# Last attention: four buffers per kind, residual two groups behind, and a wait on GpSimd every fourth group

## The chip, the cores and the metric

The kernel runs on one NeuronCore of a Trainium2 chip, alone. The metric is the device time in microseconds of one execution, the median of the runs shown. Before the change it is 2379.06 us, the median of 3 runs (2378.51 to 2380.45).

## What is computed

Four graph layers in a row on 50,000 nodes of 128 features and 25,000 edges sorted by destination. Each layer is followed by a residual sum and a layer norm, `x = layernorm(x + layer(x))`. The last layer is an attention with one head:

```
h = x @ W
alpha = leaky_relu(att_l . h[dst] + att_r . h[src])
a = exp(alpha - segment_max(alpha, dst)[dst]); a = a / (segment_sum(a, dst)[dst] + 1e-16)
out = segment_sum(h[src] * a, dst) + bias
x = layernorm(x + out)
```

## The kernel before

The kernel works on edges in NG = 49 groups of 512 (GT = 4 tiles of 128 edges), the last layer like the others. It is a row of stages with a barrier of all engines between them. In the profiled execution they lie about as follows: preparation to 68 us, stage a (gathers of source rows, statistics, first logits) to 642, softmax and b to 794, c to 1130, a softmax to 1166, d (second half of the first layer) to 1345, e (second layer) to 1674, f (third layer) to 2045, g (gathers and logits of the last layer, and the rows of nodes without edges) to 2366, and h (the last attention) to the end. Most of the change lies in stage h; the wait on GpSimd lies in the helper that stages f and h share.

In stage h each group g passes these steps, written by helpers as a software pipeline. `pipeline(eng, stages)` takes pairs (lag, step) and, for each g in order, has the engine issue every step for group g - lag in the order of the list.

- **weighing** (VectorE, L1207): the source rows times their attention weight, into `msg[:, s]`, with s = g % 2. The rows of 28 groups lie in SBUF; those of the other 21 come from DRAM through `ring`.
- **turning** (TensorE, L1334): four transposes of `msg` into `bank[s]`.
- **scanning** (VectorE, L1222): a segmented running sum from `bank[s]` into `G[:, s]`, which starts from the other slot's first column.
- **project** (TensorE, L1686 and L1690): a bias row by a matmul with one row of weights (L1686), then the sum times W3 (L1690), into `bank[2 + s]`.
- **residual** (VectorE, L1674): `z[:, s] = bank[2 + s] + rload[:, j]`, j = g % 4. The old node rows `rload` come by SP's load (L1719), issued four groups ahead once `z` has freed its slot.
- **norm_stats, norm_var** (L696, L705), ScalarE's root (L738), **norm_rate** and **norm_shift** (L714, L722), then ScalarE's apply (L742) into `outr[:, j]`, one of four output slots.
- **scatter** (GpSimd, L686): four indirect DMAs of 128 rows each, from `outr[:, j]` to the output. ScalarE writes a slot again only when the scatters of four groups earlier have landed (`h_sc{j}`).

VectorE's order of one step is scan of g, rate of g-2, weighing of g+1, shift of g-2, residual, stats and variance of g-1. TensorE's is turning of g, project of g-1. There are two slots each of `msg`, `G`, turned bank, row bank and `z`. Stage d has the same pipeline with 64 columns in place of 128, its output stored by SP and not scattered. Stage f scatters each group to a DRAM table by the same GpSimd helper `attend_pool`.

Of the kernel before, what the change touches and what calls it, by code (L numbers as in the profile page):

```python
# [15 lines left out]
P = 128  # L16
# [8 lines left out]
GT = 4  # L25
# [30 lines left out]
def program(nc, x, src, dst, ea, W1, al1, ar1, b1, W2, al2, ar2, b2, L1W, L1b,  # L56
# [21 lines left out]
    with ExitStack() as ctx:  # L78
# [182 lines left out]
        def S(name):  # L261
            return sem_of(shared(name)[0])
# [37 lines left out]
        def wait(eng, name, n):  # L300
            sem_name, start = shared(name)
            eng.wait_ge(sem_of(sem_name), n + start)
            if eng is nc.sync and not isinstance(n, int):
                pause(eng)
# [28 lines left out]
        def pipeline(eng, stages, between=(), ahead=0):  # L333


            least, most = min(lag for lag, _ in stages), max(lag for lag, _ in stages)
            parts = len(between)
            ends = {-ahead + RING * (1 + (BODIES - 1) * (n + 1) // parts): between[n] for n in range(parts)}
            for g in range(least, NG + most):
                if g in ends:  # L340
                    ends[g]()
                for lag, stage in stages:
                    if 0 <= g - lag < NG:
                        stage((g - lag) // RING, (g - lag) % RING)

        def count(eng, name, i, j, lag=0, per=1):

            n = RING * i + j + 1 - lag
            if isinstance(n, int) and n <= 0:
                return  # L350
            wait(eng, name, n * per)
# [332 lines left out]
        def scatter(pool, frm, table, kind, g, done):  # L684
            for c in range(GT):
                nc.gpsimd.indirect_dma_start(  # L686
                    table, bass.IndirectOffsetOnAxis(ap=idx[:, kind, (g + 1) * GT + c:(g + 1) * GT + c + 1].bitcast(U32), axis=0), frm(c), None,
                    bounds_check=N - 1, oob_is_err=False).then_inc(done, 16)
# [991 lines left out]
        def attend_tensor(pe, tag, width, W, b):  # L1680
            def project(i, j):
                s = j % 2
                count(pe, tag + "_scan", i, j)
                count(pe, tag + "_z", i, j, 2)
                if b:
                    nc.tensor.matmul(bank[2 + s][:], ones[0:1, 0:P], brow, start=True, stop=False)  # L1686

                k = width if b else width + 1
                for c in range(GT):
                    ins = nc.tensor.matmul(bank[2 + s][:, c * F:(c + 1) * F], G[0:k, s, c * P:(c + 1) * P], W[:],  # L1690
                                           start=not b, stop=not b or c == GT - 1)
                ins.then_inc(S(tag + "_mm"), 1)
            wait(pe, tag + "_ones", 1)
            pipeline(pe, [(0, turning(pe, tag, width)), (1, project)])
# [10 lines left out]
        def attend_pool(pool, tag, table, kind, rev):  # L1705
            def step(i, j):
                g = RING * i + j
                count(pool, tag + "_row", i, j)
                scatter(pool, lambda c: outr[:, j, c, :], table, kind, NG - 1 - g if rev else g, S(f"{tag}_sc{j}"))
            at_tiles(step)  # L1710
            for j in range(RING):
                wait(pool, f"{tag}_sc{j}", GT * 16 * (BODIES + (j == 0)))

        def linear_sync(sp, tag, table, to, rev, used, more=None, also=()):

            def load(i, j):
                g = RING * i + j
                count(sp, tag + used, i, j, RING)
                sp.dma_start(rload[:, j].rearrange("p t f -> p (t f)"), edge_row(table, NG - 1 - g if rev else g)) \  # L1719
                    .then_inc(S(f"{tag}_ld{j}"), 16)  # L1720

            def rows(i, j):

                g = RING * i + j
                if g < NR:
                    return
                if g >= NR + RING:
                    count(sp, tag + "_msg", i, j, RING)
                sp.dma_start(ringf[:, j, 0, :], edge_row(more, NG - 1 - g if rev else g)) \
                    .then_inc(S(f"{tag}_xs{j}"), 16)  # L1730

            def store(i, j):
                g = RING * i + j
                count(sp, tag + "_row", i, j)
                sp.dma_start(edge_row(to, NG - 1 - g if rev else g), outf[:, j, :]).then_inc(S(f"{tag}_out{j}"), 16)
            if more is None:
                pipeline(sp, [(-2, load)] + ([(3, store)] if to is not None else []) + list(also))
            else:
                pipeline(sp, [(-2, rows), (-2, load)])
            if to is not None:  # L1740
                for j in range(RING):
                    wait(sp, f"{tag}_out{j}", 16 * (BODIES + (j == 0)))
# [354 lines left out]
        def g_sync(sp):  # L2097
# [31 lines left out]
            for s in range(OQ):  # L2129
                sp.wait_ge(S(f"go_out{s}"), 32 * len(range(s, NQD, OQ)))  # L2130

        block = ctx.enter_context(nc.Block())

        @block.sync
# [46 lines left out]
        @block.tensor  # L2181
        def _(pe):
            prep_tensor(pe)
            barrier(pe)
            a_tensor(pe)
            barrier(pe)
            softmax_tensor(pe, 0, HEADS, feat[:, :, HF:FW], wide, None)
            b_tensor(pe)
            barrier(pe)
            c_tensor(pe)  # L2190
            barrier(pe)
            softmax_tensor(pe, 1, 1, logit[:, :, 0:1], slim, (last,), own)
            barrier(pe)
            attend_tensor(pe, "d", HF, W2_s, 0)
            barrier(pe)
            e_tensor(pe)
            barrier(pe)
            f_tensor(pe)
            barrier(pe)
            g_tensor(pe)  # L2200
            barrier(pe)
            softmax_tensor(pe, 2, 1, logit4, slim, (first,), own4)
            attend_tensor(pe, "h", P, W3_s, 1)
            barrier(pe)

        @block.scalar
# [24 lines left out]
        @block.vector  # L2231
        def _(v):
            prep_vector(v)
            barrier(v)
            a_vector(v)
            barrier(v)
            softmax_vector(v, 0, HEADS, wide, None, None, alpha[:, :, 0:HEADS])
            b_vector(v)
            barrier(v)
            c_vector(v)  # L2240
            barrier(v)
            softmax_vector(v, 1, 1, slim, (last,), None, alpha[:, :, 0:1])
            barrier(v)
            attend_vector(v, "d", feat, HF, False)
            barrier(v)
            e_vector(v)
            barrier(v)
            f_vector(v)
            barrier(v)
            g_vector(v)  # L2250
            barrier(v)
            softmax_vector(v, 2, 1, slim, (first,), 1e-16, alpha[:, :, 0:1])
            attend_vector(v, "h", None, P, True)
            barrier(v)


# [23 lines left out]
```

## Time and profile before

| | us |
|---|---|
| median of the timed runs | 2379.06 (2378.51 to 2380.45) |
| span of the profiled execution | 2740.2 |
| busy: TensorE matmuls | 1916.0 (70%) |
| busy: VectorE | 1686.4 (62%) |
| busy: GpSimd | 1374.4 (50%) |
| busy: ScalarE | 1075.7 (39%) |

The profiled execution is 361 us longer than the timed ones. Busy times are sums over a span in which the stages have different limits, so what bounds stage h has to be read from its own stretch. TensorE's ends are modelled in a profile and its starts are recorded. Where the profile can't name what ended a wait, it writes "remote" or "another core or an unknown queue"; there is only one core here.

### The profile page before, as it was taken

To read this page: it belongs to the slowest core of one execution; us is meant where nothing else is said; L and a number is where in the kernel's file an instruction comes from. 1 tells how busy PE (TensorE), PEld (TensorE's weight loads), DVE (VectorE), ACT (ScalarE), POOL (GpSimd) and SP (SyncE) were. 2 spreads that over 40 slices of the span, in tenths; PEclk is the share of its full clock that TensorE was granted. 3 is DMA by queue.
4 is the path that set the end of the run, shared out by engine and by line. 5 is a ranking of instruction groups with operands and counts; after the bars stand their busy time and mean duration, and the time that the engine had idled before them with its cause. 6 is when DMAs were issued, how large, how long until landed. Compare 5 with 4: busy or idle time off the path is not lost.

```text
span 2740.2 us, 31801 instructions
## 1 busy us (share of the span) xinstructions
PE 1916.0 (70%) x7812; PEld 1275.1 (47%) x7812; DVE 1686.4 (62%) x6502; ACT 1075.7 (39%) x2966; POOL 1374.4 (50%) x1389
## 2 busy tenths in 40 slices
PE   1788888886556776577545556999965777567573
PEld 1677777886432222166444444666541211244342
DVE  3544444446866666499657776999863655655553
ACT  0222222221654444445334443666653444232222
POOL 4566666650015555300266660677665666256555
PEclk9656555556777667555577777999985555555555
DMA  3444544445356554344466553335426887422331
GB/s 78 144 138 137 136 130 129 138 137 197 132 200 188 167 155 142 106 139 150 131 188 174 163 169 105 127 129 148 136 71 223 312 281 262 144 73 74 99 103 38
DMA packets 273498, 403.75 MB, mean 147 GB/s; under 512 B 98887, under 2 KB 115424, under 8 KB 273060
## 3 DMA queue, kind: packets, MB, share of 16 engines
q1 hardware_dynamic: 216108, 308.88, 34.9%
q0 software_dynamic: 43904, 76.05, 10.8%
q10 hardware_dynamic: 13304, 16.80, 1.7%
q8 instruction: 65, 1.06, 0.2%
q14 instruction: 117, 0.96, 0.1%
HBM read 223.76 MB, written 185.49 MB: 149 GB/s over the span
## 4 chain that ended last, share of the span: by engine, by line
DVE 21%; issue 15%; ACT 9%; PE 6%; another core or an unknown queue 6%; POOL 0%; DMA 0%; SPq 0%; ACTq 0%; DVEq 0%; POOLq 0%
ACT outr L742 4%; DVE G L1222 4%; DVE stats L696 4%; DVE msg L2048 3%; DVE z L1674 2%; ACT big L1947 2%; DVE z L1826 2%; DVE mv L705 1%; PE bank L1690 1%; ACT big L1955 1%; PE bank L1686 1%; DVE z L1834 1%; ACT hT L1933 1%; DVE xT L1523 1%
## 5 line engine op out<-in xcount | busy, mean ns | idle before, releaser
L680 POOL DMA_INDIRECT ring<-in_x_dram,idx x392 | 373.3, 952 | 228.5 <-issue 96.3
L680 POOL DMA_INDIRECT ring<-x_t,idx x280 | 268.4, 959 | 370.2 <-SPq L313 209.0
L742 ACT ACTIVATE outr<-z,rn 128x128 f32<-128x128 f32 x784 | 322.6, 483 | 252.7 <-DVE rn L722 105.4
L680 POOL DMA_INDIRECT ring<-hidden_e,idx x196 | 192.4, 982 | 303.3 <-DVE idx L1548 166.4
L686 POOL DMA_INDIRECT x_t<-outr,idx x196 | 235.3, 1201 | 172.7 <-ACT outr L742 94.1
L686 POOL DMA_INDIRECT out_dram<-outr,idx x196 | 193.6, 988 | 186.0 <-ACT outr L742 129.7
L2078 PE MATMUL bank<-DB,z 20*128 20x512 f32 x196 | 201.9, 1131 | 76.9 <-DVE xT L1523 29.7
L1106 DVE COPY cross<-bank 128x32 f32<-128x32 f32 x49 | 9.4, 191 | 318.0 <-remote 294.3
L1334 PE MATMUL bank<-ident,msg 128*64 128x128 f32 (+1 forms) x392 | 102.9, 417 | 145.7 <-DVE msg L1207 138.8
L1004 PE MATMUL bank<-bT,msg 128*128 128x4 f32 x784 | 153.1, 318 | 73.6 <-ACT msg L1046 68.0
L1690 PEld LDWEIGHTS bank<-W_s,G 65*128 65x128 f32 (+1 forms) x784 | 169.6, 318 | 69.5 <-issue 67.1
L1222 DVE TENSOR_TENSOR_SCAN G<-cont,G,bank 128x512 f32<-128x512 uint8 (+1 forms) x144 | 179.7, 1248 | 27.2 <-remote 21.6
L1004 PEld LDWEIGHTS bank<-bT,msg 128*128 128x128 f32 x784 | 147.8, 281 | 90.2 <-ACT msg L1046 84.5
L1690 PE MATMUL bank<-W_s,G 65*128 65x128 f32 (+1 forms) x784 | 187.4, 417 | 0.4 <-DVE G L1222 0.4
L696 DVE BATCH_NORM_STATS2 stats<-z 128x6 f32<-128x128 f32 x784 | 171.1, 281 | 5.1
L738 ACT ACTIVATE sd<-mv,epsc 128x4 f32<-128x4 f32 x196 | 57.8, 295 | 286.4 <-DVE mv L705 155.6
L1538 DVE SCALAR_TENSOR_TENSOR msg<-iota,shi,bank 128x391 bf16<-128x391 f16 x196 | 113.6, 619 | 91.2 <-PE bank L1498 40.1
L1674 DVE TENSOR_TENSOR z<-bank,ring 128x512 f32<-128x512 f32 x98 | 67.0, 683 | 127.2 <-remote 85.0
L1334 PEld LDWEIGHTS bank<-ident,msg 128*64 128x64 f32 (+1 forms) x392 | 64.4, 188 | 168.4 <-DVE msg L1207 152.6
L1497 PE MATMUL bank<-table,hT 128*128 128x391 bf16 x196 | 81.7, 417 | 81.4 <-issue 37.0
L1786 PE MATMUL bank<-ident,outr 128*128 128x128 f32 x196 | 41.5, 350 | 137.1 <-ACT hT L1862 56.9
L680 POOL DMA_INDIRECT big<-x_t,idx x112 | 106.6, 952 | 57.9 <-issue 31.6
(404 smaller groups left out, 4647.1 us busy)
## 6 DMA issues: line engine op xcount, KB each, us to landing
hT<-in_x_dram SPq DMA_DIRECT2D x194, 256.0 KB
x_t<-outr SPq DMA_DIRECT2D x98, 256.0 KB
ring<-x_e SPq DMA_DIRECT2D x98, 256.0 KB
x_t<-xload SPq DMA_DIRECT2D x48, 512.0 KB, 3.9
xsrc_e<-ring SPq DMA_DIRECT2D x49, 256.0 KB
xd_e<-ring ACTq DMA_DIRECT2D x49, 256.0 KB
ring<-xsrc_e SPq DMA_DIRECT2D x49, 256.0 KB
x_t<-xT SPq DMA_DIRECT2D x49, 256.0 KB
```

Source lines behind the costliest of these rows:

```text
L680: nc.gpsimd.indirect_dma_start(to(c), None, table, bass.IndirectOffsetOnAxis(ap=idx[:, kind, (g + 1) * GT + c:(g + 1) * GT + c + 1].bitcas ...
L686: nc.gpsimd.indirect_dma_start(table, bass.IndirectOffsetOnAxis(ap=idx[:, kind, (g + 1) * GT + c:(g + 1) * GT + c + 1].bitcast(U32), axis= ...
L696: ins = v.bn_stats(stats[:, k, :], z[:, s, k, :])
L742: ins = nc.scalar.activation(to[:, k, :], frm[:, k, :], ACT.Identity, bias=sc[:, k, 1:2], scale=sc[:, k, 0:1])
L1004: ins = nc.tensor.matmul(bank[4 + g % 2][:, at:at + 4], dxT[:, h, k * P:(k + 1) * P], bT[:], start=True, stop=True)
L1222: return v.tensor_tensor_scan(o, m, src_ap, ini, ALU.mult, ALU.add)
L1334: ins = nc.tensor.transpose(bank[s][0:width, c * P:(c + 1) * P], msg[:, s, c, 0:width], ident[:])
L1538: v.scalar_tensor_tensor(picked[:, c, :], iota[:], shi[:, t:t + 1], bank[t % 5][:, 0:HI], ALU.is_equal, ALU.mult, accum_out=found[:, t:t + ...
L1674: v.tensor_tensor(z[:, s], bank[2 + s][:].rearrange("p (t f) -> p t f", f=F), rload[:, j], ALU.add) \
L1690: ins = nc.tensor.matmul(bank[2 + s][:, c * F:(c + 1) * F], G[0:k, s, c * P:(c + 1) * P], W[:], start=not b, stop=not b or c == GT - 1)
L2048: c.do(v.tensor_tensor_reduce(msg[:, n, k, :], frm, attb[:, n, :], 1.0, 0.0, ALU.mult, ALU.add, dots[:, k, n:n + 1]))
L2078: nc.tensor.matmul(bank[2 + q % 4][:], ecT[q % 4], DB[0:GT * CN, :, :].rearrange("p t f -> p (t f)"), start=True, stop=True).then_inc(S("o ...
```

## The change

Stage h gets functions of its own for TensorE and VectorE. `msg`, `G`, the turned banks and the row banks have four slots each (j = g % 4; the added slots are space that `hT` left free and banks 4 to 7); `z` keeps two. VectorE's order becomes scan of g, rate of g-3, weighing of g+2, shift of g-3, residual, stats and variance of g-2. TensorE's becomes turning of g+2, project of g. SP issues the loads of the 21 groups' rows four groups ahead, which was two. GpSimd, in stage f and in stage h, waits before the scatters of groups 4, 8, ..., 48 until those of the group before have landed: 12 waits in each stage. The instructions of compute and the transfers are otherwise the same in number and shape.

```diff
@@ attend_pool
                 g = RING * i + j
                 count(pool, tag + "_row", i, j)
+                if g and g % RING == 0:
+                    wait(pool, f"{tag}_sc{RING - 1}", GT * 16 * i)
                 scatter(pool, lambda c: outr[:, j, c, :], table, kind, NG - 1 - g if rev else g, S(f"{tag}_sc{j}"))
@@ linear_sync
-                pipeline(sp, [(-2, rows), (-2, load)])
+                pipeline(sp, [(-4, rows), (-2, load)])
@@ program
+        h_msg = [msg[:, 0], msg[:, 1], dq[:, 0], dq[:, 1]]
+        h_G = [Gf[:, 0:GE], Gf[:, GE:2 * GE], dqf[:, 2, :], dqf[:, 3, :]]
+        h_turned = [bank[0], bank[1], bank[4], bank[5]]
+        h_rows = [bank[2], bank[3], bank[6], bank[7]]
+
+        def h_tensor(pe):
+            def turn(i, j):
+                count(pe, "h_msg", i, j)
+                count(pe, "h_scan", i, j, 4)
+                for c in range(GT):
+                    ins = nc.tensor.transpose(h_turned[j][:, c * P:(c + 1) * P], h_msg[j][:, c, :], ident[:])
+                ins.then_inc(S("h_tr"), 1)
+
+            def project(i, j):
+                count(pe, "h_scan", i, j)
+                count(pe, "h_z", i, j, 4)
+                nc.tensor.matmul(h_rows[j][:], ones[0:1, 0:P], brow, start=True, stop=False)
...
+            pipeline(pe, [(-2, turn), (0, project)])
+
+        def h_vector(v):
...
+            def weighed(i, j):
+                g = NG - 1 - (RING * i + j)
+                count(v, "h_tr", i, j, 4)
...
+            def summed(i, j):
+                g = RING * i + j
+                count(v, "h_tr", i, j)
+                count(v, "h_scan", i, j, 1)
+                count(v, "h_mm", i, j, 4)
+                ini = h_G[(j - 1) % RING][:, 0:1] if g else 0.0
+                v.tensor_tensor_scan(h_G[j][:, ::-1], cont[:, g * GE:(g + 1) * GE], h_turned[j][:, ::-1], ini,
+                                     ALU.mult, ALU.add).then_inc(S("h_scan"), 1)
+
+            def residual(i, j):
+                count(v, "h_mm", i, j)
+                wait(v, f"h_ld{j}", 16 * (i + 1))
+                count(v, "h_row", i, j, 2)
+                v.tensor_tensor(z[:, j % 2], h_rows[j][:].rearrange("p (t f) -> p t f", f=F), rload[:, j], ALU.add) \
+                    .then_inc(S("h_z"), 1)
+            pipeline(v, [(0, summed), (3, norm_rate(v, "h")), (-2, weighed), (3, norm_shift(v, "h")), (2, residual),
+                         (2, norm_stats(v, "h")), (2, norm_var(v, "h"))])
@@ block.tensor
-            attend_tensor(pe, "h", P, W3_s, 1)
+            h_tensor(pe)
@@ block.vector
-            attend_vector(v, "h", None, P, True)
+            h_vector(v)
```

## Rows read from the trace of the kernel before

**Rows 1.** The page: the span, and its line of DVE, groups by idle time before them.
```profile
span 2740.2 us, 31801 instructions
L1106 DVE COPY cross<-bank 128x32 f32<-128x32 f32 x49 | 9.4, 191 | 318.0 <-remote 294.3
```

**Rows 2.** Busy time by stretch: stages a, c, e and the attention of h.
```profile
core 0: us, PE busy (x) PEld busy (x) DVE busy (x) ACT busy (x) POOL busy (x), PEclk, DMA share, GB/s
76.00:606.00 530.00, 452.50 (x2304) 407.87 (x2305) 224.63 (x1492) 119.83 (x309) 342.65 (x360) 0.60 0.48 134
810.00:1130.00 320.00, 225.78 (x619) 76.41 (x618) 203.80 (x613) 154.46 (x516) 184.78 (x188) 0.71 0.56 162
1349.00:1645.00 296.00, 146.98 (x880) 130.41 (x881) 193.35 (x735) 119.45 (x295) 188.55 (x196) 0.73 0.61 171
2403.00:2731.00 328.00, 212.32 (x650) 129.67 (x648) 178.89 (x614) 93.39 (x240) 193.56 (x196) 0.55 0.26 80
```

**Rows 3.** Who waited for whom, 2403 to 2731: us in total, times, longest.
```profile
POOL out_dram L686 <- ACT outr L742: 129.7, 12, 51.7
DVE z L1674 <- remote: 85.0, 10, 11.2
POOL out_dram L686 <- issue: 56.4, 184, 0.5
```

**Rows 4.** Timeline, one stall of stage h: start us, us, instruction, idle before.
```profile
2439.75 2.07 PE L1686 MATMUL bank<-xlast,ones 1*128 1x512 f32 x2
...
2444.61 2.07 PE L1686 MATMUL bank<-xlast,ones 1*128 1x512 f32 x2
...
2446.61 2.08 PE L1690 MATMUL bank<-W_s,G 128*128 128x128 f32 x8
...
2454.36 0.98 POOL L686 DMA_INDIRECT out_dram<-outr,idx  x1 [0.30 <-issue]
2455.64 0.98 POOL L686 DMA_INDIRECT out_dram<-outr,idx  x1 [0.30 <-issue]
2457.54 0.69 DVE L1674 TENSOR_TENSOR z<-bank,ring 128x512 f32<-128x512 f32 x1 [9.77 <-remote]
...
2461.47 1.65 ACT L742 ACTIVATE outr<-z,rn 128x128 f32<-128x128 f32 x4 [1.59 <-DVE rn L722]
...
2463.91 0.98 POOL L686 DMA_INDIRECT out_dram<-outr,idx  x1 [7.28 <-ACT outr L742]
...
2483.22 0.98 POOL L686 DMA_INDIRECT out_dram<-outr,idx  x1 [0.30 <-issue]
2485.10 0.69 DVE L1674 TENSOR_TENSOR z<-bank,ring 128x512 f32<-128x512 f32 x1 [9.77 <-remote]
```

**Rows 5.** Busy time by stretch, columns as in 2: across the same stall.
```profile
2446.00:2449.60 3.60, 3.60 (x14) 2.66 (x13) 1.76 (x4) 1.86 (x5) 2.69 (x4) 0.50 0.36 118
2449.60:2452.00 2.40, 2.15 (x10) 1.20 (x10) 0.00 (x0) 0.00 (x0) 1.79 (x3) 0.99 0.10 29
2452.00:2457.50 5.50, 0.00 (x0) 0.00 (x0) 0.00 (x0) 0.00 (x0) 3.71 (x4) 0.60 0.16 52
```

**Rows 6.** Timeline of stage d: the same pipeline without scatters.
```profile
1240.88 0.68 DVE L1674 TENSOR_TENSOR z<-bank,ring 128x512 f32<-128x512 f32 x1
...
1244.03 0.39 DVE L1207 TENSOR_TENSOR msg<-big,alpha 128x256 f32<-128x256 f32 x1
...
1244.41 0.68 DVE L1674 TENSOR_TENSOR z<-bank,ring 128x512 f32<-128x512 f32 x1
```

**Rows 7.** Groups of VectorE by line, 2403 to 2720: count, busy us, mean ns, idle.
```profile
L1207 DVE TENSOR_TENSOR msg<-big,alpha 128x512 f32<-128x512 f32 x24 | 15.9, 662 | 0.0
```

**Rows 8.** Half microseconds around the last scatter's transfer, columns as in 2.
```profile
2456.50:2457.00 0.50, 0.00 (x0) 0.00 (x0) 0.00 (x0) 0.00 (x0) 0.12 (x1) 0.50 0.00 0
2457.00:2457.50 0.50, 0.00 (x0) 0.00 (x0) 0.00 (x0) 0.00 (x0) 0.00 (x0) 0.50 0.34 111
2457.50:2458.00 0.50, 0.00 (x0) 0.00 (x0) 0.46 (x1) 0.00 (x0) 0.00 (x0) 0.50 0.00 0
```

**Rows 9.** Timeline of stage f: ScalarE's apply and GpSimd's scatters.
```profile
1802.77 1.64 ACT L742 ACTIVATE outr<-z,rn 128x128 f32<-128x128 f32 x4
...
1802.98 1.24 POOL L686 DMA_INDIRECT x_t<-outr,idx  x1 [0.30 <-issue]
...
1805.18 1.73 POOL L686 DMA_INDIRECT x_t<-outr,idx  x1 [0.96 <-issue]
...
1811.99 1.73 POOL L686 DMA_INDIRECT x_t<-outr,idx  x1 [0.96 <-issue]
```

**Rows 10.** Timeline, start of stage h's attention.
```profile
2396.49 0.69 DVE L1674 TENSOR_TENSOR z<-bank,ring 128x512 f32<-128x512 f32 x1 [2.14 <-PE bank L1690]
```

More of the change, by code:

```diff
@@ L2130, in g_sync @@
                 sp.wait_ge(S(f"go_out{s}"), 32 * len(range(s, NQD, OQ)))
+        h_msg = [msg[:, 0], msg[:, 1], dq[:, 0], dq[:, 1]]
[13 more added lines that the diff above has]
+                nc.tensor.matmul(h_rows[j][:], ones[0:1, 0:P], brow, start=True, stop=False)
+                for c in range(GT):
+                    ins = nc.tensor.matmul(h_rows[j][:, c * F:(c + 1) * F], h_G[j][:, c * P:(c + 1) * P], W3_s[:],
+                                           start=False, stop=c == GT - 1)
+                ins.then_inc(S("h_mm"), 1)
+            wait(pe, "h_ones", 1)
+            pipeline(pe, [(-2, turn), (0, project)])
@@ new lines, in h_vector @@
+        def h_vector(v):
+            v.tensor_copy(brow.rearrange("p (t f) -> p t f", f=F), bias[0:1, 3:4, :].to_broadcast([1, GT, F])) \
+                .then_inc(S("h_ones"), 1)
+            def weighed(i, j):
+                g = NG - 1 - (RING * i + j)
+                count(v, "h_tr", i, j, 4)
+                if g < NG - NR:
+                    wait(v, f"h_xs{j}", 16 * len(range(j, RING * i + j + 1, RING)[(NR - j + RING - 1) // RING:]))
+                v.tensor_tensor(h_msg[j], g_rows(g) if g >= NG - NR else ring[:, j, 0],
+                                alpha[:, four(g), 0:1].to_broadcast([P, GT, F]), ALU.mult).then_inc(S("h_msg"), 1)
+            def summed(i, j):
[14 more added lines that the diff above has]
+                         (2, norm_stats(v, "h")), (2, norm_var(v, "h"))])
```

## Prediction

> **What bounds the kernel now.** I read first the page's span against the median [rows 1]: the profiled execution takes 2740.2 us, the timed ones 2379.06. The 361 us between them are 15%, so it matters where they lie before any stall of the profile is believed. Then the waits of stage h [rows 3], where two entries stand out: VectorE's residual waits 85.0 us in 10 times for something the profile cannot name, and GpSimd waits 129.7 us for ScalarE, of which 51.7 are the wait for the first group and 78.0 the 11 others. The timeline of one stall [rows 4] shows how they belong together. TensorE's product for the residual of group 9 starts at 2446.61 and runs 2.08 us, to 2448.69, but the residual that reads it starts at 2457.54. In between only GpSimd works: its last scatter ends at 2456.62 (2455.64 + 0.98), and 0.92 us later the residual goes. The next such residual, at 2485.10, again starts 0.90 us after the last scatter's end (2483.22 + 0.98 = 2484.20). The cycle is 2485.10 - 2457.54 = 27.56 us for four groups, against 16 scatters x (0.98 + 0.30) = 20.5 us of GpSimd's work; the rest is its wait of 7.28 us less rounding.
>
> So the cause seems to be that TensorE's "done" reaches VectorE late while GpSimd issues without a pause. That TensorE itself was not late is seen by stretch [rows 5]: it is busy to about 2451.8, its granted clock goes to 0.99 of full speed after the dense stretch, which is the 2.4 GHz level, and falls back during the 5.5 us in which it does nothing. It had finished and gone idle; only the message was late.
>
> Is this there in the timed runs? The stages in which GpSimd issues without a pause beside a dense TensorE are a, c, e and h. Their idle time of GpSimd beyond its own pace [rows 2], each scatter or gather taken with 0.30 us of issue: a 530 - (342.65 + 360 x 0.30) = 79, c 320 - (184.78 + 188 x 0.30) = 79, e 296 - (188.55 + 196 x 0.30) = 49, h 328 - (193.56 + 196 x 0.30) = 76. Together 283 us: were all of it gone in the timed runs, 2740 would become 2457, still above 2379. In stage a alone VectorE waits 294.3 us for the nameless source [rows 1]. Were instead the stalls as long in the timed runs, the whole 361 us would have to come from rows that look regular: stage d, with the same pipeline and no scatters, runs one group in 1244.41 - 1240.88 = 3.53 us without any idle time in these rows [rows 6]. I therefore take it as likelier that TensorE's late messages are an effect of recording, and that in the timed runs stage h goes at the pace of its slowest engine.
>
> Those paces, per group: GpSimd 4 x 1.28 = 5.13 us [rows 4]; TensorE 2444.61 - 2439.75 = 4.86 us at the 1.2 GHz level [rows 4]; VectorE 3.53 us of stage d plus the wider weighing, 0.66 - 0.39 = 0.27 us, which is 3.80 us [rows 6, 7]. GpSimd bounds, and TensorE is 5% behind.
>
> **The change part by part.**
>
> Four slots and the residual two groups behind. The work of VectorE and TensorE is the same in count and shape. Both engines have slack to GpSimd (1.33 and 0.27 us per group), so looser coupling between them gains 0 where GpSimd bounds. If GpSimd did not bound, TensorE at 4.86 us would, and in the rows it already goes without gaps between stalls [rows 4]; more buffers give it nothing. The first group's way to its scatter keeps its length: its residual waits for TensorE's first product [rows 10]; one turning stands between the first scan and that product before (of group 1) and after (of group 2), and each waits for a weighing beside that scan. I take 0, with 1 us as the bound either way.
>
> SP's loads four groups ahead. A load of rows for group g+4 waits for the weighing of g, and the residual's loads stand behind it on the same queue. That weighing is done two of VectorE's steps earlier than what SP waits for next, so nothing is held up. No wait for a load is among the stage's large entries [rows 3]: 0.
>
> GpSimd's 12 waits in stage h. Each holds the next group's four scatters, and nothing else is queued behind it on that engine; ScalarE waits for these scatters only four groups later. The price is the time from the start of the group's last scatter to its landing, plus the restart, less the 1.28 us at which the next would have followed. Landing: the last scatter starts at 2455.64 [rows 4], its data moves between 2457.0 and 2457.5, and nothing moves after that [rows 8]. The signal thus comes not before 1.36 us after the start, and I bound it at 2458.0, 2.36 us after; I take 2.0. Restart: ScalarE's apply ends at 2461.47 + 1.65 = 2463.12 and GpSimd starts at 2463.91 [rows 4], so 0.79 us. One wait costs 2.0 + 0.79 - 1.28 = 1.5 us, from 0.9 to 1.9. Twelve cost 18 us, from 10 to 23, all of it on the path if GpSimd bounds. What could hide it is the group pace of the others: four groups take TensorE 19.4 us and GpSimd 20.5, then 22.0. The price falls once 16 scatters take GpSimd less than 19.4 us in the timed runs (5% faster than here), and is nothing below 19.4 - 1.5 = 17.9 us (13% faster).
>
> The Trainium skill ("DMA: Bandwidth & Descriptors", Anatomy of one DMA) puts such a DMA at 2.0 us plus its bytes by 436 GB/s. For 64 KB this gives an estimate of 2.15 us to landing, and 1.66 us per wait, 20 us in all where the rows give 18; the bounds above hold it.
>
> GpSimd's 12 waits in stage f. There one group takes 1811.99 - 1805.18 = 6.81 us, and the first scatter follows the apply's end, 1804.41, by 0.77 us: GpSimd waits for ScalarE and is idle 0.96 us per group [rows 9]. By the same 2.0 + 0.79 us from 1802.98 the scatter would start at 1805.77 and not 1805.18, 0.6 us late, and the next group's idle time takes that in. If that cover were gone it would be 7 us; I take 1 us for the last group.
>
> Sum: 0 + 0 + 18 + 1 = 19 us. It is a difference, and I add it to the median, since the profiled span holds the stalls that I take for absent: 2379 + 19 = 2398 us. In the profiled execution I expect another sign, see below.
>
> **The rivals.**
>
> The stalls are real, and the change removes them (faster). Then GpSimd's new pause of 1.5 us in each four groups is what lets TensorE's messages through before the whole pipeline runs dry, since they go 0.9 us after it stops, and the deeper buffers keep work in stock. The cycle of 27.56 us falls towards 20.5 + 1.5 = 22.0 us. VectorE has 4 x 3.80 = 15.2 us to do in the part of the cycle that is not stalled, 22.0 - 9.77 = 12.2 us, so it will not get all the way; I take 24. That is 12 x 3.6 = 43 us, and 2336 us; at the floor 12 x 5.56 = 67 us and 2312. For it speaks how exactly the stalls end with GpSimd's bursts [rows 4]; against it, the 361 us. The Trainium skill ("Perfetto Trace Analysis", Optimization Strategy) says that the same gap repeating on an engine can mean too few buffers for the next tile. By that rule buffers alone would close the 9.77 us gaps and the time would go to the same 2312 to 2336 us; the rows speak against a lack of buffers as the first cause, as what the residual reads was computed 8.8 us before.
>
> No change that can be measured. GpSimd is so much faster in the timed runs that its pause fits below TensorE's 19.4 us, or a part of real stalls pays for it: within 0.2%, 2379 us. For it speaks that 283 us of stalls do not fill the 361 us, so some 78 us more are due to recording and may lie in GpSimd's 1.28 us.
>
> **How the numbers follow.** The forecast, slower by 10 to 23 us: 0.48. Real stalls removed: 0.34. No measurable change: 0.17, and 0.01 for anything else. A measurement of this kernel can tell about 0.2%, or 4.8 us, from no change. The range reaches from 2328, which leaves out the deepest third of the faster case (0.12), to 2404, above which I leave 0.04. As cases of both signs hold most of the chance: the likeliest one's own range is 2389 to 2402.
>
> **What would show it.** In the profile after: pauses of about 2.8 us from the start of the last scatter of groups 3, 7, ... to the next start, where it was 1.28; if they are longer than 3.3 us the price was too low. In stage f no change of pace. In the profiled execution, where the stalls are, I expect a shorter stage h by about 40 us while the timed runs get slower: both signs at once would be the strongest support for recording as their source. If timed runs and profiled span fall together, the stalls are real and the step that dates them to recording is wrong. If the timed runs do not move and the pauses are there, GpSimd was not the bound.

## The result, and the profile after

The changed kernel takes 2407.14 us (median of 4 runs, 2403.61 to 2412.59), beside 2378.78 us of the kernel before (2375.63 to 2380.45). The ratio is 1.0127, with an interval from 1.0111 to 1.0143: slower by 28 us. The direction is the forecast's; the size is half as much again as its 19 us, and the median lies 3 us above the range.

The page of the kernel after, its span and its line of GpSimd's output scatters, and its groups of VectorE by line (this one line answers to that of [rows 1]):

```profile
span 2404.4 us, 31821 instructions
...
L686 POOL DMA_INDIRECT out_dram<-outr,idx x196 | 196.4, 1002 | 130.6 <-issue 57.5
```

```profile
L1106 DVE COPY cross<-bank 128x32 f32<-128x32 f32 x49 | 8.1, 166 | 38.3 <-PE bank L1004 38.3
```

The profiled execution is now 2 us shorter than its own timed one (2406.27), where that of before was 361 us longer than the median. The nameless waits are gone in every stage, also in stage a, which the change doesn't touch: 294.3 us of "remote" [rows 1] have become 38.3 us of waiting for TensorE. So this profile can't be laid beside the one of before line by line. The experiments say why; a profile of the kernel before that can be compared is shown with the first of them.

Stage h's attention after, busy time by stretch (columns as in rows 2) and who waited for whom on GpSimd (us in total, times, longest):

```profile
2110.50:2395.00 284.50, 204.97 (x632) 123.31 (x631) 175.87 (x607) 88.70 (x239) 196.41 (x196) 0.56 0.29 91
```

```profile
POOL out_dram L686 <- issue: 57.5, 183, 2.1
POOL out_dram L686 <- ACT outr L742: 45.0, 2, 42.9
POOL out_dram L686 <- DMA out_dram<-outr,idx: 28.1, 11, 3.8
```

Apart from the wait for the first group (42.9 us), GpSimd waits for ScalarE once more and hardly at all. All the rest of the stretch is its own issuing and the new waits for scatters to land. One short and one long pause, in the timeline of GpSimd and of SP's queue (start us, us, instruction, idle before):

```profile
2152.73 0.98 POOL L686 DMA_INDIRECT out_dram<-outr,idx  x1 [0.30 <-issue]
...
2154.37 0.32 SPq L1721 DMA_DIRECT2D ring<-x_e  x1
...
2155.82 0.98 POOL L686 DMA_INDIRECT out_dram<-outr,idx  x1 [2.10 <-DMA out_dram<-outr,idx]
...
2157.11 1.43 POOL L686 DMA_INDIRECT out_dram<-outr,idx  x1 [0.30 <-issue]
...
2175.58 0.98 POOL L686 DMA_INDIRECT out_dram<-outr,idx  x1 [0.30 <-issue]
...
2176.06 0.32 SPq L1721 DMA_DIRECT2D ring<-x_e  x1
...
2179.82 0.98 POOL L686 DMA_INDIRECT out_dram<-outr,idx  x1 [3.26 <-DMA out_dram<-outr,idx]
...
2181.10 1.44 POOL L686 DMA_INDIRECT out_dram<-outr,idx  x1 [0.30 <-issue]
```

From start to start the short pause is 2155.82 - 2152.73 = 3.09 us and the long one 2179.82 - 2175.58 = 4.24 us, where scatters otherwise follow each other by 1.29. The twelve of the stage, read in the same way, are 3.07, 3.09, 4.24, 3.09, 3.10, 4.26, 3.06, 4.78, 4.21, 3.12, 3.00 and 2.95: eight short ones of 3.06 on average, four long ones of 4.37. Together they are 42.0 us, which is 42.0 - 12 x 1.29 = 26.5 us more than without waits. Two things that the prediction didn't have come on top. The second scatter after a pause is busy for 1.30 to 1.45 us and not 0.98 in 8 of the 12 cases, 3.5 us in all. And after one pause the second scatter starts 3.07 us after the first (the 2.1 us of "issue" above), 1.8 us more. 26.5 + 3.5 + 1.8 = 31.8 us. The kernel before has 3.6 us of slower scatters of its own (in its trace beside 2377 us, below), which leaves 28 us for the change: what the timed runs show.

### The profile page after: what moved, and what is told of

It is laid out like the page before. It is cut to its first block, busy times and chain, and to the rows that moved or that the text cites. A ratio compares the mean times of both kernels' runs of the same rounds, so it can differ in the third digit from the quotient of the medians.

```text
span 2404.4 us, 31821 instructions
## 1 busy us (share of the span) xinstructions
PE 1814.1 (75%) x7812; PEld 1215.4 (51%) x7812; DVE 1677.6 (70%) x6502; ACT 1080.3 (45%) x2966; POOL 1377.2 (57%) x1389
## 4 chain that ended last, share of the span: by engine, by line
POOL 19%; DVE 13%; issue 12%; ACT 8%; DMA 4%; PE 3%; POOLq 1%; SPq 0%; DVEq 0%; ACTq 0%
POOL ring L680 9%; POOL out_dram L686 5%; POOL big L680 4%; DVE stats L696 4%; ACT outr L742 3%; DVE G L1222 2%; ACT big L1949 2%; DMA ring<-x_t,idx 2%; DVE mv L705 1%; DVE z L2019 1%; DMA out_dram<-outr,idx 1%; DVE z L1674 1%; ACT big L1957 1%; ACT hT L1935 1%; DVE msg L2050 1%
## 5 line engine op out<-in xcount | busy, mean ns | idle before, releaser
L1089 DVE BATCH_NORM_STATS2 stats<-ring 128x6 f32<-128x128 f32 x196 | 42.6, 280 | 191.7 <-DMA ring<-in_x_dram,idx 191.6
L1046 ACT ACTIVATE msg<-bank 128x512 f32<-128x512 f32 x98 | 58.6, 598 | 203.5 <-PE bank L994 203.5
L1004 PE MATMUL bank<-bT,msg 128*128 128x4 f32 x784 | 137.3, 298 | 0.7 <-ACT msg L1046 0.7
L2050 DVE CUSTOM_DVE_ANT_0 msg<-ring,attb 128x128 f32<-128x128 f32 x280 | 64.1, 288 | 102.4 <-DMA ring<-x_t,idx 59.7
L1921 PE MATMUL bank<-MmMs,G 128*128 128x256 f32 x392 | 121.5, 392 | 6.1 <-DVE z L2019 3.3
L714 DVE RECIPROCAL rn<-sd 128x4 f32<-128x4 f32 x196 | 33.0, 168 | 130.6 <-ACT sd L738 129.8
L1222 DVE TENSOR_TENSOR_SCAN G<-cont,G,bank 64x512 f32<-64x512 uint8 (+1 forms) x96 | 119.6, 1245 | 3.0 <-PE bank L1761 1.7
L1497 PE MATMUL bank<-table,hT 128*128 128x391 bf16 x196 | 72.1, 368 | 53.2 <-DVE hT L1532 53.0
L1016 PE MATMUL bank<-ident,ring 128*128 128x128 f32 x392 | 86.2, 386 | 29.7 <-DMA ring<-in_x_dram,idx 29.6
L742 ACT ACTIVATE outr<-z,est 128x128 f32<-128x128 f32 x196 | 80.5, 486 | 43.2 <-DVE z L1555 42.8
```

Of the source, the lines that this page charges most:

```text
L742: ins = nc.scalar.activation(to[:, k, :], frm[:, k, :], ACT.Identity, bias=sc[:, k, 1:2], scale=sc[:, k, 0:1])
L1004: ins = nc.tensor.matmul(bank[4 + g % 2][:, at:at + 4], dxT[:, h, k * P:(k + 1) * P], bT[:], start=True, stop=True)
L1016: ins = nc.tensor.transpose(bank[2 + n][:, c * P:(c + 1) * P], ring[:, g % RING, n, c, :], ident[:])
L1222: return v.tensor_tensor_scan(o, m, src_ap, ini, ALU.mult, ALU.add)
L1497: nc.tensor.matmul(o, lhs, table[:, 0, :], start=True, stop=False)
L1921: nc.tensor.matmul(o[:, 0:2 * F], G[:, s, e], MmMs[:], start=True, stop=False)
```

## The experiments

The runs were made on four chips. On two of them, one used at two different times, the kernel before took 2376 to 2378 us beside them; on the two others it took 2748 and 2779 us. Which chip gave the result, and which the profile of [rows 1], isn't on record. The first experiments were to find which part costs what.

**The kernel before, once more.** No edit.

> The kernel before, unchanged, for a second profile. Theory (the 361 us by which its first profile was longer are an effect of recording that comes and goes): either again about 2740 us, or, as in the profile of the changed kernel, a span within 5 us of the timed runs with stage h at about 303 us from the barrier to the end and no nameless waits of 9.8 us. Rival (the stalls belong to the kernel before in every profile and the change removes them): again 2740 us with stalls in stage h, while the other three kernels of this call, which share its stages a to g, show none there.

2382.38 us in one run, beside a median of 2377.3 (2374.65 to 2380.21, 19 runs). The page, VectorE's groups by line, the stretch of stage h and GpSimd's waits in it:

```profile
span 2380.5 us, 31801 instructions
```

```profile
L1106 DVE COPY cross<-bank 128x32 f32<-128x32 f32 x49 | 8.0, 163 | 35.2 <-PE bank L1004 35.1
```

```profile
2115.50:2371.50 256.00, 199.59 (x645) 122.61 (x643) 179.29 (x610) 89.79 (x239) 196.08 (x196) 0.60 0.33 102
```

```profile
POOL out_dram L686 <- issue: 57.9, 190, 0.3
POOL out_dram L686 <- ACT outr L742: 44.7, 6, 43.1
```

The same program, profiled, has a span 360 us shorter than in [rows 1], 2 us below its own timed run, and no stall. So recording need not lengthen it. Whether it does so now and then, which was expected too, this one run can't tell; but the kernel before timed at 2748 us, below, shows that timed runs can be as long as that first profile. Laid beside the first profile, from the first indirect DMA of a stage to its last, this one is shorter by 88 us in a, 67 in c, 48 in e, 42 in g and 72 in h, and equal in f (336 us in both); the other 41 us lie between the stages. The prediction had a, c, e and h at 79, 79, 49 and 76 and left out g.

The semaphore events that both traces hold say the same of TensorE. Of its 97 completions in stage h all have their event within 1.5 us of the start of the last matmul here, mostly 0.43 us after it. In the first profile 60 of the 97 have none in that time, and that for the residual at 2457.54 [rows 4] stands at 2457.51, 9.2 us after the last matmul for it began (2448.27). Events can be missing from a record; the one at 2457.51 is there, and late.

And the stretch of this profile shows what bounds stage h here: 196 scatters x 1.29 = 253 of its 256 us are GpSimd's, which waits for ScalarE hardly but at the first group (43.1 of 44.7 us).

**The buffers alone.** The changed kernel without

```diff
-                if g and g % RING == 0:
-                    wait(pool, f"{tag}_sc{RING - 1}", GT * 16 * i)
```

> The changed kernel with its GpSimd wait taken out of both stages; the four slots, the residual two groups behind and the earlier row loads stay. Theory (GpSimd's issue bounds stage h, the wait is the whole loss): 2379 us as before, within 4 us, and GpSimd issues 196 scatters of stage h in about 252 us from first start to last end. Rival (the buffers or the longer software pipeline cost something): 2390 us or more. Rival (the buffers gain and the wait eats the gain): under 2370 us.

2374.79 us (2372.82 to 2379.57, 10 runs), ratio 0.9994 (0.9985 to 1.0004): no difference. From first scatter to last, stage h takes 253.5 us.

**The wait alone, in stage h.** The kernel before with

```diff
+                if tag == "h" and g and g % RING == 0:
+                    wait(pool, f"{tag}_sc{RING - 1}", GT * 16 * i)
```

> The kernel before with nothing but the wait, in stage h alone: 12 waits. Theory: all of the loss, 2379 + 28 = 2407 us, from 2402 to 2412; start-to-start over a pause 3.1 to 4.3 us where it was 1.29. Rival (the wait is cheap and the buffers cost): under 2390 us.

2408.22 us (2405.19 to 2411.49), ratio 1.0126 (1.0107 to 1.0144). That is the whole loss of the change, and leaves nothing for stage f's twelve waits, nor for the buffers.

**A wait for older scatters.** In the changed kernel, `RING - 1` becomes `RING - 2`: GpSimd waits as often, but for the scatters of two groups before.

> The changed kernel, but the wait is for the scatters of two groups earlier, which have landed by then if GpSimd is the bound and its queue in order. Theory (what costs is the landing of the last scatter): 2379 to 2384 us. Rival (the wait instruction itself, or a restart of GpSimd, costs): 2400 us or more.

2375.72 us (2374.2 to 2378.2, 10 runs), ratio 0.9992 (0.9982 to 1.0001). GpSimd's waits for landing in stage h:

```profile
POOL out_dram L686 <- DMA out_dram<-outr,idx: 1.8, 6, 0.3
```

No pause is over 1.29 us. The instruction of the wait costs nothing; what costs is to stand until the last scatter has landed.

**Where the kernel before takes 2748 us.** These four were laid out by the numbers above and ran where the kernel before, beside them, took 2747.73 us (2742.06 to 2753.18, 13 runs). Twice as many waits:

```diff
-                if g and g % RING == 0:
-                    wait(pool, f"{tag}_sc{RING - 1}", GT * 16 * i)
+                if g and g % 2 == 0:
+                    wait(pool, f"{tag}_sc{(g - 1) % RING}", GT * 16 * ((g - 1) // RING + 1))
```

> The changed kernel with the wait before every second group, 24 waits in each of stages f and h. Theory (each wait costs stage h its landing and restart, 2.4 us as 12 of them cost 29 in all): 2377 + 58 = 2435 us, from 2428 to 2445, and stage f unchanged within 3 us, as its GpSimd has 0.96 us to spare per group. Rival (a fixed cost of having waits, or a price that overlap hides when they come often): 2420 us or less. Rival (stage f loses its cover at this rate): 2448 us or more, with stage f longer by 5 us or more.

2748.3 us, ratio 1.0 (0.9983 to 1.0017). The changed kernel with the residual's loads of stage h done only for the first four groups, for which alone VectorE then waits:

```diff
@@ load
+                if tag == "h" and g >= RING:
+                    return
@@ residual
-                wait(v, f"h_ld{j}", 16 * (i + 1))
+                wait(v, f"h_ld{j}", 16)
```

> The changed kernel with its 12 waits, but in stage h the residual's node rows are loaded for the first four groups alone and used again after that (that work is left out, so the residual of the other groups is of other rows). Theory (a landing takes 2.2 us alone and 3.4 us when one of these loads is moved in front of it): the pauses before groups 4 to 28 are all 3.1 us from start to start, none of 4.2 us; the time falls by the four or five long pauses, to 2400 to 2404 us. Rival (the long landings have another source): pauses of 4.2 us remain and the time stays within 2 us of 2407.

2714.84 us, ratio 0.9901 (0.9865 to 0.9938). Three scatters per group in place of four in stage h, on the kernel before and on the changed one without its waits:

> The kernel before with one of the four scatters of each group of stage h left out (a quarter of the rows is not written). GpSimd then needs 3 x 1.29 = 3.86 us per group and can be under the others. Theory (two slots each; TensorE next at up to 4.86 us per group at the 1.2 GHz level): 2345 to 2365 us. Rival (GpSimd still bounds): 2377 - 63 = 2314 us.

> The four slots and the residual two groups behind without any wait, and one of four scatters left out as in the run beside it. Theory (buffers gain nothing, whatever bounds): within 5 us of the run beside it. Rival (the two slots do couple TensorE and VectorE, and it shows once GpSimd no longer covers it): 10 us or more below it, down to 2314 us where GpSimd bounds again.

2654.13 us, ratio 0.9658 (0.9625 to 0.9691), and 2662.92 us, ratio 0.9697 (0.9654 to 0.974). All four expectations were written for 2377 us and missed in absolute terms. As ratios they say something else: 24 waits, which should cost tens of microseconds, cost nothing here. These times fit the profile of before (span 2740.2), so the question became whether the change itself is a gain there.

**The change and its two parts, where the kernel before takes 2779 us** (2771.09 to 2785.25, 8 runs).

> The changed kernel, unchanged. On one chip the kernel before took 2377 us, on another 2748 us with the stalls in stages a, c, e and h that its first profile shows. Theory (the late messages of TensorE belong to the chip, not to recording, and where they occur the pause of GpSimd lets them through): beside a kernel before of about 2377 us it is 28 us slower; beside one of about 2748 us it is 35 to 50 us faster, stage h's scatters in about 285 us where they took 328. Rival (the change is slower on any chip by its 12 pauses): 28 us slower beside either.

> The kernel before with the 12 waits in stage h alone. Theory: 28 us slower beside a kernel before of 2377 us. Beside one of 2748 us the pause alone gives at least half of the gain, 20 us or more faster. Rival (only the four slots together with the wait gain there): within 5 us of 2748.

> The four slots without a wait. Theory: within 4 us of the kernel before beside 2377 us. Beside 2748 us within 10 us of it, since what is late is the message and no buffer: the stalls of 9.8 us stay. Rival (too few buffers make the bubbles there): 30 us or more faster.

> The kernel before with one of the four scatters of each group of stage h left out (a quarter of the rows is not written). Theory beside 2377 us (GpSimd bounds stage h by its issue, the next is TensorE at up to 4.86 us per group): 2345 to 2365 us; were GpSimd still the bound, 2314 us. Beside 2748 us as in its run there, about 94 us faster.

Changed kernel 2739.07 us, ratio 0.9868 (0.9826 to 0.9909); wait alone 2760.4, ratio 0.9938 (0.9917 to 0.996); buffers alone 2760.1, ratio 0.9925 (0.9896 to 0.9954); three scatters 2677.91, ratio 0.9636 (0.9611 to 0.966). In microseconds: the wait 19 faster, the buffers 19 faster, both together 40. The change gains within its expected 35 to 50; each part alone gains about half, which for the buffers is more than the 10 us expected. The stretches of stage h, of the changed kernel, the wait alone and the buffers alone in this order, and VectorE's nameless waits and GpSimd's waits for ScalarE in it, of the changed kernel:

```profile
2433.20:2730.30 297.10, 193.54 (x632) 117.18 (x632) 175.10 (x607) 93.09 (x240) 193.96 (x196) 0.59 0.29 88
```

```profile
2423.90:2737.60 313.70, 202.41 (x650) 123.41 (x648) 179.32 (x616) 93.38 (x240) 195.43 (x196) 0.58 0.27 84
```

```profile
2426.50:2749.30 322.80, 197.50 (x646) 120.05 (x644) 175.43 (x613) 93.38 (x240) 193.80 (x196) 0.59 0.26 81
```

```profile
POOL out_dram L686 <- ACT outr L742: 82.3, 11, 51.5
...
DVE z L2183 <- remote: 70.3, 13, 11.4
```

The kernel before wasn't profiled on this chip. Its first profile has 328 us in that stretch [rows 2] and 85.0 us of nameless waits [rows 3], but it may come from another chip, so the comparison is rough: by it the stretch is 31 us shorter with the change (285 us were expected, 297 measured), 14 with the wait and 5 with the buffers, so of the latter's 19 us most isn't seen there. The stalls don't vanish, they become fewer: beyond the first group GpSimd waits for ScalarE 82.3 - 51.5 = 30.8 us, where it was 78.0.

How the wait helps isn't shown. If its pauses let TensorE's messages through, VectorE's long waits should end in them. In the trace of the changed kernel six waits of the residual are longer than 8 us; two end within 0.4 us of a pause of 2.1 us (at 2528.17 and 2578.22), the other four while GpSimd issues.

**The questions of the second group, again where the kernel before takes 2378 us** (2377.99; 2370.76 to 2381.3, 11 runs). Twice as many waits:

> The changed kernel with the wait before every second group, 24 waits in stage f and in stage h. Theory beside a kernel before of 2377 us (each wait costs 2.4 us): 2435 us, from 2428 to 2445. Rival (a price that does not grow with the number): 2420 us or less. Beside 2750 to 2780 us: level with before, as in its first run.

2451.37 us (2446.05 to 2452.95), ratio 1.0302 (1.0276 to 1.0328): slower by 73 us, more than either number expected. GpSimd's waits in stage h:

```profile
POOL out_dram L686 <- DMA out_dram<-outr,idx: 68.5, 24, 3.7
```

Its 24 pauses are 92.5 us from start to start; less 24 x 1.29 that is 61.5 us, and slower second scatters with one late one, as above, add 9. Against the kernel before, which has slower scatters too, stage h is longer by 67 us from first scatter to last (322.9 for 255.5), 2.8 us per wait. Stage f is longer by 4.6 us (340.5 for 335.9), so its spare time no longer covers all of its 24 waits: the third number of the first run's expectation, 2448 us or more, is the one that fits. The price of a wait isn't fixed: 16 of the 24 are long ones here, over 3.4 us.

Without the residual's loads after the first four groups:

> The changed kernel with its 12 waits, in stage h the residual's node rows loaded for the first four groups alone (that work is left out). Theory beside 2377 us (a landing takes 2.2 us alone and 3.4 us when such a load is moved in front of it): the pauses before groups 4 to 28 are all 3.1 us from start to start, and the time is 2400 to 2404 us. Rival (the long landings have another source): pauses of 4.2 us remain, 2405 us or more.

2407.96 us (2406.89 to 2408.97), ratio 1.0126 (1.0103 to 1.0149): no gain on the changed kernel. The pauses are 3.09, 3.10, 3.08, 3.08, 3.58, 3.10, 3.28, 6.25, 4.31, 3.01, 2.99, 2.95, together 41.8 us against 42.0. The two before groups 12 and 24, long with the loads (4.24 and 4.26), are short without them, as the theory had it; one before group 20 is now 3.58. Those before groups 32 and 36, where SP issues loads of the 21 groups' rows, stay long, and the first of them is longer by 1.5 us. So the long pauses of the earlier groups go with the residual's loads, but the total doesn't hang on these loads alone, and the forecast of the time missed.

Three scatters of four, without waits:

> The four slots and the residual two groups behind without a wait, one of the four scatters of each group of stage h left out. Theory beside 2377 us (GpSimd bounds by its issue; TensorE at up to 4.86 us per group is next): 2345 to 2365 us. Rival (with a quarter of its work gone GpSimd still bounds): 2314 us.

2309.58 us (2309.15 to 2312.44), ratio 0.9717 (0.9694 to 0.9739). The stretch and GpSimd's waits:

```profile
2108.00:2301.00 193.00, 169.84 (x651) 104.63 (x649) 175.60 (x616) 94.15 (x242) 144.22 (x146) 0.70 0.41 124
```

```profile
POOL out_dram L686 <- ACT outr L742: 47.4, 5, 43.3
POOL out_dram L686 <- issue: 42.8, 140, 0.4
```

The theory expected TensorE to take over as the bound. It doesn't, and the rival's 2314 us is near: the stretch is still 147 scatters x 1.29 = 190 us and the rest of the waits are trifles. TensorE does the same work with a mean granted clock of 0.70 of full speed, where it was 0.60 beside GpSimd's longer stretch, and gets along with less than 193 / 49 = 3.94 us per group. Its 4.86 us [rows 4] were read at the 1.2 GHz level and are no floor.

**A pause that waits for nothing.** In place of the wait, a memset on GpSimd that writes nothing anybody reads:

```diff
+                if tag == "h" and g and g % RING == 0:
+                    if i > 1:
+                        pool.wait_ge(S("h_fill"), i - 1)
+                    nc.gpsimd.memset(xload[:], 0.0).then_inc(S("h_fill"), 1)
```

> The changed kernel with its waits in both stages taken out, and in their place in stage h a fill of unused memory on GpSimd (1024 values per partition, 0.95 us in another stage) before groups 4, 8, ..., 48: a pause of issuing without a wait for a landing. Theory (what costs is the length of the pause, 2.4 us of it per landing): beside a kernel before of 2377 us it costs 12 x 0.95 = 11 us, 2385 to 2391. Beside one of about 2750 to 2780 us: if a short pause in issuing is enough to let TensorE's messages through, 45 us or more faster. Rival there (it is the landing, not the pause, that lets them through): as the buffers alone, about 20 us faster.

2387.19 us (2382.14 to 2389.74, 8 runs), ratio 1.0036 (1.0023 to 1.005). In the timeline:

```profile
2152.27 0.98 POOL L686 DMA_INDIRECT out_dram<-outr,idx  x1 [0.31 <-issue]
2153.24 0.98 POOL L1712 MEMSET xload<- 128x1024 f32 x1
2154.38 0.98 POOL L686 DMA_INDIRECT out_dram<-outr,idx  x1 [0.17 <-issue]
```

A gap is 2.11 us where it was 1.29: 12 x 0.82 = 10 us, and the time rises by 9. The same once more, and with the memset before each second group, 24 times; the kernel before took 2376.1 us beside them (2370.15 to 2381.2, 7 runs):

> The changed kernel with 12 fills of unused memory on GpSimd in stage h, each a pause of 0.83 us in issuing, and no wait for a landing. Theory beside a kernel before of about 2750 to 2780 us: a pause of under 1 us is shorter than the 0.9 us after which TensorE's messages went there, so it lets few through, about as the buffers alone, 15 to 25 us faster. Rival there (any pause is enough): as the change itself or better, 37 us or more faster. Beside 2377 us: 9 us slower again.

> The same with a fill before every second group, 24 in stage h. Theory beside 2377 us (each pause costs its own length, 0.83 us): 18 us slower, 2392 to 2400 us. Beside 2750 to 2780 us: twice the chances for the messages; if short pauses let them through at all, more of a gain than with 12, otherwise less by the 10 us that the further pauses take.

2387.55 us, ratio 1.0046 (1.0029 to 1.0063), and 2398.96 us (2397.16 to 2400.89), ratio 1.0089 (1.0072 to 1.0106): 11 and 23 us, for 10 and 20 us of added gap; from first scatter to last stage h is longer by 8 and 21 us (263.6 and 276.4 for 255.5). On such a chip each microsecond in which GpSimd issues nothing in stage h is one of the kernel's time. These two were meant for a chip with stalls, to see whether any pause lets the late messages through; they met none, and that question stays open.

## Why the prediction was right or wrong

**GpSimd bounds stage h, the buffers give nothing: right** where the kernel before takes 2377 us. The stretch is its 196 scatters by 1.29 us, the buffers alone measure 0.9994, and added gaps come back one for one. The step about TensorE being 5% behind was wrong (three scatters of four), without harm to the sum.

**Twelve waits in h at 1.5 us: the term that was mis-sized.** 18 us were put down, with 23 at most; the runs show 28 to 31 for it, 2.5 us each. The eight short pauses cost 3.06 - 1.29 = 1.77 us each, inside the bounds of 0.9 to 1.9. Their parts: the landing (the scatter's semaphore in the trace) comes 2.1 to 2.3 us after the last scatter's start, mostly 2.24, where 2.0 was taken from half-microsecond rows [rows 8], and GpSimd restarts 0.84 us later, where it was 0.79. The step that failed is the landing's upper bound, 2.36 us: in the four long pauses it comes 3.4 to 3.9 us after the start, and each costs 3.08 us. The slower scatters after a pause, 3.5 and 1.8 us, were in no term. The bounds came from one scatter whose landing fell into a moment in which no other transfer moved [rows 8], during a stall. While the pipeline runs, SP's loads move on the same DMA engines. In the long pause above a load of 256 KB is issued at 2176.06, 0.5 us after the last scatter's start, and the busy share of the DMA engines is 0.93 and 0.43 in the two microseconds in which the landing is awaited. In the short pause the load is issued at 2154.37, 1.6 us after the start, and the share is 0.17:

```profile
2154.00:2155.00 1.00, 1.00 (x5) 0.67 (x5) 0.96 (x5) 0.00 (x0) 0.00 (x0) 0.50 0.17 57
```

```profile
2177.00:2178.00 1.00, 1.00 (x3) 0.50 (x2) 1.00 (x5) 0.00 (x0) 0.00 (x0) 0.50 0.93 160
2178.00:2179.00 1.00, 1.00 (x2) 0.00 (x0) 0.51 (x1) 0.00 (x0) 0.00 (x0) 0.50 0.43 162
```

All twelve pauses of this trace sort in the same way: in the four long ones SP issues a load 0.48 or 0.49 us after the last scatter's start, in the eight short ones 0.82 us after it or later, or none. With 24 waits 15 of the 16 long pauses have a load issued 0.40 to 0.53 us after, and no short one has. That such a load makes the pause long is read from these traces; the one run made for it took the residual's loads away, which shortened the pauses before groups 12 and 24 and left the sum. Nor is it the only source: in the run of the wait alone two long pauses, 4.20 and 3.78 us, have no load in front.

By the Trainium skill ("DMA: Bandwidth & Descriptors", Anatomy of one DMA), 2.0 us plus bytes by 436 GB/s, an estimate for 64 KB is 2.15 us; the 2.24 us of a landing that had the engines to itself agree with it. For the 3.4 us and more that sum has no term.

**Twelve waits in f at 1 us: right** within what can be told. The wait alone in stage h already has the whole loss, and stage f takes 336.8 us from first scatter to last after, 335.9 before and 334.8 with the buffers alone. Of the trace after, the first scatters of three groups and the last before the wait, which the next group's idle time takes in:

```profile
1549.74 1.73 POOL L686 DMA_INDIRECT x_t<-outr,idx  x1 [0.96 <-ACT outr L742]
...
1554.35 1.24 POOL L686 DMA_INDIRECT x_t<-outr,idx  x1 [0.30 <-issue]
1557.67 0.98 POOL L686 DMA_INDIRECT x_t<-outr,idx  x1 [2.08 <-DMA x_t<-outr,idx]
...
1563.35 1.73 POOL L686 DMA_INDIRECT x_t<-outr,idx  x1 [0.58 <-issue]
```

The second group starts 1563.35 - 1549.74 = 13.61 us after the first one shown, which is twice the 6.81 us of a group: the 1.1 us by which the wait delays the one between are made up.

**The stalls as an effect of recording: wrong**, and the most instructive step. The argument was sound as far as it went: a span 361 us over the median can't be the execution that was timed. But of the two ways to explain this, the prediction weighed only what recording does. The other is that profile and times come from different conditions. The same program takes 2377 us timed and 2380.5 profiled on one chip, 2748 and 2779 timed on two others, and the 2740.2 of the profile of before fits those. There the late messages are real and are timed too: the profiles taken on these chips have the nameless waits and spans 2 us below their own times. The sign test announced for it (timed slower, profiled span shorter, "the strongest support for recording") did come out, with 2740.2 against 2404.4, and would have misled: the span fell by 336 us, eight times the 40 us that were expected, because the profile after is from an execution without stalls. Only the kernel before, profiled again beside its own time and timed on other chips, settled it. One reading of rows was loose as well: between 2448.69 and 2457.54 not only GpSimd works, TensorE does too until 2451.8 [rows 5].

**The rival with real stalls: right in sign and close in size, on the one chip with stalls where it was run; its mechanism is not shown.** It gave 43 us; measured are 40, from 2779.01 to 2739.07. Its reasons were two, the pause that lets messages through and the deeper stock of work, and each part alone gives about half (19 and 19 us). But stage h has stalls left, and most of the long waits end outside the pauses, so how near 43 comes to 40 is in part luck. Its place in the chances, 0.34, stood for a doubt about conditions that no row of a single trace could remove. The rule from the Trainium skill ("Perfetto Trace Analysis", Optimization Strategy), that a repeating gap can mean too few buffers, gets 19 us there, not the 43 to 67 that it was given, and nothing on the other chips.

**No change at all** fell with GpSimd's pace: 1.29 us in an undisturbed execution against 1.28 in the disturbed one. The 78 us that the prediction left unexplained are not in it: they lie in stage g (42 us) and between the stages.

No version beats both kernels everywhere: the buffers alone, and the wait for older scatters, are level with the kernel before at 2377 us; the former gains 0.75% at 2779 us, and the latter wasn't run there.

## What to carry to other kernels

When a profile's span doesn't fit the timed median, profile the same kernel again beside its own time before explaining the gap, and don't compare the span of a change with a span from elsewhere. A wait for a DMA's landing on the engine that bounds a stage costs latency and restart each time, here 1.8 us where the DMA engines were free and 3 us where they weren't; bound it with rows from a moment in which the other queues are running. Waiting for the transfers of one turn earlier cost nothing here.

## What the runs showed of the hardware

- Four chips, one program: 2376 to 2378 us on two, 2748 and 2779 on the others, each within 0.4% of its own median. The difference shows in stages in which GpSimd issues indirect DMAs without pause, as waits of VectorE for TensorE's completion of up to 11 us; in the stall of [rows 4] the work was done 8.8 us before. Stage f, where GpSimd waits for ScalarE in each group, takes 336 us in either kind. What makes a chip do so is open, and so is whether it stays so: the two slow ones were used once each.
- An indirect DMA of 128 rows (64 KB) keeps GpSimd busy 0.98 us and the next follows 1.29 us after its start; the second one after a pause of 3 us or more takes about 1.44 us in most cases (7 of 12, and 16 of 24). Why is open.
- Such a scatter lands 2.1 to 2.3 us after its start in the eight short pauses, and 3.3 to 3.9 us in 19 pauses in which SP issued a load of 256 KB 0.40 to 0.53 us after that start.
- GpSimd issues 0.84 us after the landing it waited for.
- With a quarter of the scatters gone, TensorE's mean granted clock in the same work rose from 0.60 to 0.70 of full speed, and its 4.86 us per group, read at 1.2 GHz, proved to be no floor.
